# A two-layer attention and expert kernel: silu from ScalarE's table for the first layer's gates, three in one slot

## The reference, cut to what matters

```
def _L0_ffn_ref(x, w_gate, w_up, w_down):
    wg = _dequant(w_gate, x.dtype)
    wu = _dequant(w_up, x.dtype)
    wd = _dequant(w_down, x.dtype)
    gate = jnp.einsum('bsd,hd->bsh', x, wg)
    up = jnp.einsum('bsd,hd->bsh', x, wu)
    h = jax.nn.silu(gate) * up
    return jnp.einsum('bsh,dh->bsd', h, wd)
...
xn = _layernorm(x, axis=-1)
x = x + _L0_attn_ref(xn, ...) + _L0_ffn_ref(xn, L0_ffn_w_gate, L0_ffn_w_up, L0_ffn_w_down)
xn = _layernorm(x, axis=-1)
x = x + _L1_attn_ref(xn, ...) + _L1_ffn_ref(xn, ...)
```

## Time and profile before

| | us |
|---|---|
| median of 3 runs | 647.14 |
| lowest and highest run | 646.85, 649.95 |
| the profiled execution's own time | 649.82 |
| its span, first to last instruction | 648.1 |
| TensorE busy | 563.7 (87%) |
| VectorE busy | 509.8 (79%) |
| ScalarE busy | 340.1 (52%) |
| GpSimd busy | 121.5 (19%) |

### The profile page before, as it was taken

How to read it: one execution, slowest core, us unless ns; L and a number is a source line. 1 busy time by engine, 2 the same in 40 slices (tenths; PEclk the granted TensorE clock), 3 DMA queues, 4 the chain that set the end, 5 groups by cost and what they waited for, 6 DMA issues and landing times.

```text
span 648.1 us, 10352 instructions
## 1 busy us (share of the span) xinstructions
PE 563.7 (87%) x3834; PEld 226.0 (35%) x3834; DVE 509.8 (79%) x890; ACT 340.1 (52%) x402; POOL 121.5 (19%) x209
## 2 busy tenths in 40 slices
PE   4173789799889988989999999999999999999996
PEld 2020122142124223313454435353444343445443
DVE  4497679989986987897878888979888988774443
ACT  2000576666686665665535455545455545555562
POOL 6424061232314022221112020220001000000000
PEclk9655799999999998998999999999999999999999
DMA  2698726005302541445013331025050000000000
GB/s 69 159 185 126 237 86 123 2 30 122 49 1 98 56 45 13 110 44 53 2 51 70 33 39 18 2 99 51 3 67 0 3 1 0 19 2 17 1 1 17
DMA packets 125220, 34.08 MB, mean 53 GB/s; under 512 B 103458, under 2 KB 123442, under 8 KB 124338
## 3 DMA queue, kind: packets, MB, share of 16 engines
q1 hardware_dynamic: 125170, 33.41, 28.0%
HBM read 18.05 MB, written 13.63 MB: 49 GB/s over the span
## 4 chain that ended last, share of the span: by engine, by line
PE 59%; DVE 20%; SPq 7%; issue 5%; DMA 5%; ACT 4%; POOL 1%; ACTq 0%; DVEq 0%
PE ps L535 11%; PE ps L506 11%; DVE mx L797 10%; PE ps L545 9%; PE ps L536 8%; PE ps L490 7%; PE ps L475 4%; SPq L333 3%; DVE xs L852 3%; PE ps L438 2%; DMA QO<-mT 2%; DVE th L818 2%; SPq L321 2%; PE ps L559 2%; DVE h_T L831 2%
## 5 line engine op out<-in xcount | busy, mean ns | idle before, releaser
L683 ACT ACTIVATE PT<-ps 128x1024 f32<-128x1024 f32 x256 | 260.4, 1024 | 221.1 <-PE ps L490 219.6
L797 DVE TENSOR_REDUCE mx<-ps 128x2 f32<-128x1024 f32 x256 | 307.6, 1220 | 51.0 <-PE ps L475 49.7
L506 PE MATMUL ps<-PT,Vp 128*32 128x512 f32 x1024 | 138.1, 612 | 0.4 <-ACT o_sb L689 0.4
L475 PE MATMUL ps<-KO,QO 48*128 48x512 bf16 (+1 forms) x512 | 103.6, 406 | 33.2 <-DMA KO<-z 13.6
L490 PE MATMUL ps<-QO,KO 59*128 59x512 bf16 x512 | 101.1, 391 | 18.9 <-DMA QO<-mT 14.5
L818 DVE SCALAR_TENSOR_TENSOR th<-th,ps 128x512 f32<-128x512 f32 x76 | 52.1, 686 | 48.1 <-ACT th L698 47.0
L490 PEld LDWEIGHTS ps<-QO,KO 59*128 59x128 bf16 x512 | 24.7, 93 | 167.7 <-issue 85.3
L535 PE MATMUL ps<-xnT,eg 128*128 128x512 f32 x128 | 72.0, 644 | 10.6 <-DVE mx L797 10.2
L545 PEld LDWEIGHTS ps<-ed,h_T 128*128 128x128 f32 x512 | 62.1, 192 | 16.0 <-issue 14.8
L536 PE MATMUL ps<-xnT,eu 128*128 128x512 f32 x128 | 65.6, 594 | 0.0
L545 PE MATMUL ps<-ed,h_T 128*128 128x128 f32 x512 | 62.4, 275 | 0.3 <-DVE h_T L831 0.3
(11 more groups left out here) (134 smaller groups left out, 389.8 us busy)
## 6 DMA issues: line engine op xcount, KB each, us to landing
z<-part SPq DMA_DIRECT2D x16, 384.0 KB, 2.6
z<-part SPq DMA_DIRECT2D x16, 256.0 KB, 2.9
QO<-z SPq DMA_DIRECT2D x64, 48.0 KB, 2.7
KO<-z SPq DMA_DIRECT2D x64, 48.0 KB, 2.7
QO<-z SPq DMA_DIRECT2D x6, 384.0 KB, 7.3
KO<-z SPq DMA_DIRECT2D x6, 384.0 KB, 9.2
z<-part SPq DMA_DIRECT2D x16, 128.0 KB, 2.7
QO<-mT SPq DMA_DIRECT2D x96, 4.0 KB
```

Of the source, the lines that this page charges most:

```text
L475: mm = pe.matmul(ps[:, 2 * pair + half, :], rows_of(QO[u % 3], half, 2 * s + jj, rows, (qt, qt + 1)), rows_of(KO[u % 3], half, 2 * s + jj, ...
L506: last = pe.matmul(ps[32 * g:32 * g + 32, PV_BANK, :], Vp[u % 3][:, k, head(s, g), :], PT[:, (2 * t + g % 2) % 4, g // 2, :], start=(s % 2 ...
L683: act.activation(PT[:, e % 4], ps[:, 2 * pair:2 * pair + 2, :], ACT.Exp).then_inc(exp_done, 1)
L797: dve.tensor_reduce(mx[:, a, qt, col:col + 5:4], ps[:, 2 * pair:2 * pair + 2, :], AX_X, ALU.max, negate=True).then_inc(max_read, 1)
```

## The change

Two things change, both for the first layer only. The three gates of a unit all stand in slot 9, one behind another, on each engine and in the list `taken`. The function on ScalarE is Silu itself, from its activation table, so that VectorE is left with a single multiplication by the up product; the wait for gate_done between the two passes goes too. The second layer keeps tanh and its two passes.

```
-        def gate_at(u, slot):
+        def gates_at(u, slot):
             if layer(u) == 1:
-                return SLOTS_U * seq(u) + slot
-            return HB * seq(u) + slot - 9 if 9 <= slot < 9 + HB else None
+                return [SLOTS_U * seq(u) + slot]
+            return range(HB * seq(u), HB * seq(u) + HB) if slot == 9 else []
...
-                if gate_at(u, slot) is not None:
-                    gate_up(pe, u, gate_at(u, slot))
+                for g in gates_at(u, slot):
+                    gate_up(pe, u, g)
...
-            act.activation(th[:, g % 2, :], ps[:, 2 * pair_of(f"gate{L}", g), :], ACT.Tanh, scale=0.5).then_inc(
-                tanh_done[L], 1)
+            if L == 0:
+                act.activation(th[:, g % 2, :], ps[:, 2 * pair_of("gate0", g), :], ACT.Silu).then_inc(tanh_done[0], 1)
+            else:
+                act.activation(th[:, g % 2, :], ps[:, 2 * pair_of("gate1", g), :], ACT.Tanh, scale=0.5).then_inc(
+                    tanh_done[1], 1)
...
-            dve.scalar_tensor_tensor(out=t, in0=t, scalar=1.0, in1=ps[:, bank, :], op0=ALU.add,
-                                     op1=ALU.mult).then_inc(gate_done[L], 1)
-            dve.wait_ge(gate_done[L], g + 1)
+            if L == 1:
+                dve.scalar_tensor_tensor(out=t, in0=t, scalar=1.0, in1=ps[:, bank, :], op0=ALU.add,
+                                         op1=ALU.mult).then_inc(gate_done[L], 1)
+                dve.wait_ge(gate_done[L], g + 1)
...
-            dve.scalar_tensor_tensor(out=dst, in0=t, scalar=0.5, in1=ps[:, bank + 1, :], op0=ALU.mult,
-                                     op1=ALU.mult).then_inc(h_ready[L], 1)
+            if L == 0:
+                dve.tensor_tensor(dst, ps[:, bank + 1, :], t, ALU.mult).then_inc(h_ready[0], 1)
+            else:
+                dve.scalar_tensor_tensor(out=dst, in0=t, scalar=0.5, in1=ps[:, bank + 1, :], op0=ALU.mult,
+                                         op1=ALU.mult).then_inc(h_ready[1], 1)
```

More of the change, by code:

```diff
@@ L255, in build @@
                         taken.append(("max", pairs_at(u, slot)[jj]))
-                if gate_at(u, slot) is not None:
-                    taken.append((f"gate{layer(u)}", gate_at(u, slot)))
+                for g in gates_at(u, slot):
+                    taken.append((f"gate{layer(u)}", g))
                 if expert_at(u, slot) is not None:
@@ L736, in scalar_unit @@
                     output_copy(act, u, 0)
-                if gate_at(u, slot) is not None:
-                    half_tanh(act, layer(u), gate_at(u, slot))
+                for g in gates_at(u, slot):
+                    half_tanh(act, layer(u), g)
         def last_scalar(act):
@@ L964, in vector_unit @@
                     advance(40)
-                if gate_at(u, slot) is not None:
-                    gated(dve, u, gate_at(u, slot))
+                for g in gates_at(u, slot):
+                    gated(dve, u, g)
                 if expert_at(u, slot) is not None:
```

## The result

The changed kernel takes 650.51 us in the median of 20 runs, the one before 648.85 in as many: a ratio of 1.0025, 95% interval 1.0013 to 1.0036. That is 1.6 us more (0.8 to 2.3), which is within the 0.5% called no change, and not zero. The two errors, with opposite signs, largely cancel by luck.

The account below looks back on a forecast made before the run. No engine was saturated throughout; the chain of waits to each unit's maxima copy set the time. Adding 3 x 0.76 and 0.6, or 2.9 us, gave 652.7 against the profiled execution, 650.0 us as median; range 646.3 to 655.8.

Parts of the forecast that it names:

- The two errors: Forecast of 2.9 us more against 1.6 measured; its base, a median of three runs, was 1.7 below that of twenty.
- No engine saturated; the copy decides.: Units 0 to 3: the next unit starts 5.4 us after the maxima copy, so the change moves that distance four times.
- TensorE gains and loses nothing in the burst.: Slot 9: gates 1.91 us apart, two of them 1.91 earlier than before, slot 10's first score at 102.97.
- the walk: Working through slots 9 to 14 with piece durations from the profile; stated error 0.2 us a unit, 0.8 in all.
- the burst's 0.50 a unit: Units 0 to 2: the copy comes 0.50 us later from the three-gate burst alone, without any table load.
- The 2.9: Forecast total of added time in us: 3 x 0.76 for units 0 to 2 plus 0.6 for unit 3.
- VectorE loses what it gains.: Slot 9's burst: 2.1 us of passes saved in a unit, 2.87 us idle around the three multiplications.
- Two loads a unit.: Each 1.28 us: the first covered by gates, the second delays slot 10's first exponential by 0.7, 6.9 behind the first gate.
- A switch costs twice its load: Rival, chance 0.22: between third silu and slot 10's first exponential a switch takes 2.6 us; 7.9 more, 655.0 us.
- The saved passes reach the end: Rival, chance 0.07: VectorE's twelve saved passes of 0.71 us pay in full, 8.5 us less, 638.6.
- The loads don't happen or hide: Rival, chance 0.10, no change: loads cost nothing, only the burst is left, 2.1 us more, 649.2.
- TensorE's clock: Granted clock stays at 1.00 in units 0 and 3; a fall to 1.2 GHz in slots 10 to 12 would break TensorE's durations.

Follow-up runs that it names:

- The two bursts, with one and with two passes: Three gates in slot 9 with tanh, no table loads, against the kernel before: one VectorE pass gave ratio 1.0023, both passes 1.0038.
- the gates spread out: Gates in slots 9, 10 and 11, as before, with one VectorE pass: tanh gave ratio 0.9949 to before, silu with 24 table loads 1.0151.
- the four kernels that take the change apart: Against before: slot 9 burst with tanh, two passes 1.0038, one pass 1.0023; slots 9, 10, 11 with one pass, tanh 0.9949, silu 1.0151.
- extra switches: The changed kernel plus two four-element activations behind each first-layer unit's third silu, so four table loads a unit: ratio 1.0352 to before, 22.8 us slower.

## Why the prediction was right, point by point

- **No engine saturated; the copy decides.** Right for what the change does, since its gates stand ahead of the copy: behind the copy units 0 and 1 take 24.57 and 24.48 us after, 24.57 and 24.49 before. That the next unit starts 5.4 us after the copy "whatever TensorE has done meanwhile" is too strong: with the gates in slot 15 the distances of units 0 and 1 fell by over 4 us and the stretches behind them rose by as much.
- **TensorE gains and loses nothing in the burst.** This step failed. I took 1.91 for each gate from a gate that follows bf16 products. In the burst the spacings are 1.82, 1.72 and 1.81, so three gates take 5.35 instead of 5.73. So slot 10's first score comes 0.38 earlier than the walk had it, and all that follows with it. With these spacings the walk gives 0.12 in units 0 to 2 instead of 0.50 for the burst alone (measured 0.18, 0.19, 0.09) and 0.37 instead of 0.76 with the loads (measured 0.50, 0.49, 0.40); in unit 3 0.25 instead of 0.6 (measured 0.27). **The mis-sized term is the burst's 0.50 a unit.** The sum becomes 1.4 instead of 2.9, against 1.66 in the distances and 1.6 in the runs. The 2.9 was so near the 3.2 from which the forecast would have spoken of a change that it gave "same" 0.47 and "slower" 0.46, and choosing between them was partly luck; with the spacing right there would have been little doubt.
- **VectorE loses what it gains.** Right in units 0 to 2; in unit 3 it keeps 0.44 of the 2.1. Its idle times around the three multiplications are 1.26, 0.26 and 1.02, 2.54 in all where 2.87 was worked out (the gates came closer together), against 2.1 saved. The two bursts, with one and with two passes, agree to 0.01 in three units.
- **Two loads a unit.** Right. Both are 1.28, each with 0.02 beside it; the first costs nothing, and the first exponential of slot 10 comes 6.50 behind the first gate (104.58 - 98.08), 6.9 expected, 0.4 less for the same reason as the burst. The cost, 0.26 in the walk, was 0.31 to 0.33, and nothing in unit 3 (0.01).
- **A switch costs twice its load** (0.22): wrong. ScalarE starts the load 0.02 behind a running exponential's end. The Trainium skill's drain of some 1380 ns (ScalarE: Activation LUTs, What ACT_TABLE_LOAD costs) isn't seen at any of the switches in these rows; its 1283 ns for the load is.
- **The saved passes reach the end** (0.07): wrong in the burst (0.46 of 8.5), a third right with the gates spread out (2.8).
- **The loads don't happen or hide** (0.10): they happen, and 0.96 of their 10.2 us is paid.
- **TensorE's clock**: at 1.00 in the windows of units 0 and 3 after, as said. The forecast looked at units 0 and 3 from slot 9 on and passed over two dips in the clock's row: the first 8 in it (243 to 259 us) is the start of unit 3, the second (292 to 308 us) the start of unit 4. The second is there in the page after too, the first isn't.

One stretch is left out of the comparisons above except where it is named: from unit 2's copy to unit 3's slot 6, where SyncE issues the second layer's reads. It takes 28.14 before and 26.79 after, and 26.58 to 27.98 in the four kernels that take the change apart. The first maximum that needs those reads waits for the last of them (before, then after), and the windows behind it are at different clocks (columns as above):

```profile
246.42 0.47 PE L475 MATMUL ps<-KO,QO 56*128 56x512 bf16 x2 [2.10 <-DMA QO<-mask_q]
248.82 0.39 PE L475 MATMUL ps<-KO,QO 56*128 56x512 bf16 x2 [2.29 <-DMA QO<-mask_q]
...
246.42:248.42 2.00, 2.00 (x10) 0.29 (x10) 1.38 (x3) 0.00 (x0) 0.00 (x0) 0.55 0.01 4
248.82:250.82 2.00, 2.00 (x15) 0.51 (x16) 1.47 (x4) 0.25 (x1) 0.00 (x0) 1.00 0.02 4
```

From that maximum to slot 6's copy it is 8.26 us before and 6.72 after. The other kernels with all gates ahead of the copy fall into the same two groups: 8.23 to 8.32 at the lower clock (one pass in the burst, both kernels with the gates spread out), 6.71 at the full one (two passes in the burst, extra switches). So 1.5 us of this stretch go by whether TensorE came back from that wait at the lower clock, and the profile of before is one of those that did. All three kernels with the gates spread out came back low and three of the four with the burst in slot 9 at full clock; seven profiles can't tell whether the place has a part in that. The runs speak against it: their 1.6 us is what the distances alone give, and with 1.5 us regularly saved here it would be near nothing.

## What to carry to other kernels

A table load of ScalarE costs what is uncovered of it at its place: the same 1.28 cost 0.12 behind a burst of matmuls, 0.5 when each gate had its own pair, and more than its own length where TensorE ran dry and came back at the lower clock (2.6 us for each load added in units 0 to 2, with the small activation that forced it). Batching work to save switches moves the other engines' work too, so look at what the batch makes the busiest engine wait for: here three saved VectorE passes were worth nothing inside the batch in three units of four. And before an operation is made cheaper, ask if it can stand behind the point that the next stage waits for: moving two of three tanh gates unchanged behind that copy gave 1.1%, where silu in one pass gave nothing. Not all of them, though: of the work moved behind the point, what is more than the wait there is paid again (2.3 us for two gates, 4.4 for three).

## What the runs showed of the hardware that was not expected

- A 128x512 float32 product (two instructions in the rows) takes 0.86 us right behind another float32 one, and 1.06 to 1.11 behind bf16 products (chain rows above and the earlier trace rows).
- After 3.32 us without a matmul TensorE came back at a granted clock of 0.50 and kept it for about 6 us; after the 1.4 us waits at a unit's start it did not fall. The length of the wait alone does not decide: at unit 3's start the granted clock was 0.50 behind a wait of 1.61 us (gates spread out, one pass) and 1.00 behind one of 2.29 us (the changed kernel). Extra waits ahead of TensorE are therefore not linear in their length.
- At one place of one program 1.5 us went by that clock alone (8.26 us before, 6.72 after, with the same instructions); so a difference of this size between two profiles is looked for there first.
